# Float16 denominators with the queries split on GpSimd, and the output's sums of squares moved behind the split of qz

## Chip, cores and metric

One core of a Trainium2 chip. The metric is the device time of one execution in microseconds, lower is better; the kernel before takes 2459.85 us (median of three runs, 2457.72 to 2460.81). Engines are named as in the profile: PE is TensorE, PEld its weight load, DVE VectorE, ACT ScalarE, POOL GpSimd, SP the queue of SyncE.

## What is computed

x has 2 sequences of 4096 rows and 512 columns. First a linear attention with 16 heads of 32 columns, then a gated linear attention (GLA) with 8 heads of 64 and four sparse "experts"; both sit between layer norms and add to x.

```python
# first half, per head (d = e = 32, n = 4096)
q = relu(xn @ Wq.T); k = relu(xn @ Wk.T); v = xn @ Wv.T
ksum = k.sum(over n)
z = 1.0 / (einsum('bhd,bhdn->bhn', ksum, q) + eps)
context = einsum('bhdn,bhen->bhde', v, k)
out = einsum('bhde,bhen->bhdn', context, q) * z
x = x + layernorm(out @ Wproj.T + bproj)
# second half, per head, chunks of 64 rows: o = GLA(q1,k1,v,gk1) + sum over experts GLA(q2*e, k2*e, v, gk2*mask)
o = o * rsqrt(mean(o * o, axis=-1) + EPS) * norm_w
o = o * silu(g)
x = x + layernorm(o @ Wo)
```

The change touches the denominators ksum . q of the first half and the place of mean(o * o) in the second.

## The kernel before

A first stage (up to some 535 us) goes over 64 tiles of 128 rows in groups of four: layer norm, keys, queries and the moments that the context is made from. The queries, after their relu, are stored to q_cols in HBM as float32. Products of float32 accuracy with float16 operands are made by the helper `mm3` (L317 to L321): both operands are held as a high and a low float16 half, and three products (high-high, high-low, low-high) are added up in PSUM.

Between the stages VectorE makes `kden`: for each group of 128 columns the sums of the keys, spread over a block-diagonal 128x128 matrix in float32 (`key_totals`, `key_blocks`, L1463 to L1475). The weights of the mixing (`mix`) come from the context.

The second stage (from some 565 us to the end) goes over the 64 tiles again, in steps written out by hand for each engine (a `step` function per engine; loops of two steps). In step n, TensorE issues in this order: v of tile n, the sparse products of the GLA state for tile n-1 (`inter_sparse`, L494), the gates (L366), the dense ones and the intra-chunk products of n-1 (L503, L514), q1, k2, the output gate and k of n, then **the denominators of tile n+2** (`den`, L323 to L332), the output projection of tile n-2, the cumulated gates (L428, L429), q2, the half sums (L436, L438), **y of tile n+2** (`y_mm`, L334 and on; first instruction L336), the transposes of the gated q and k (L447), the state products (L466, L474), the routing and low-rank products of tile n+1 (a third use of `mm3`, 24 products of 128x128 by 128x128 for the low rank), and the scores of n (L457).

The way from the denominators to y, all of tile n+2 within step n: `den` on TensorE writes PSUM bank 0; ScalarE takes the logarithm and the exponential of it (`ahead_z`, L726 and L728); VectorE multiplies queries, key sums and that (`ahead_qz`, L1359) and splits the product into float16 halves (`ahead_qz_split`: L1181, L1183); `y_mm` reads those.

VectorE's order in a step: carries (L1220, L1229), router (L1264 and on), masks of the scores (L1200, L1208), masks of the cumulation, the low half of the low-rank values (L1255 to L1258), selection (L1239, L1242), join (L1247), log-sigmoids (L1298), maximum and difference for the softmax of k2 (L1319, L1325), `back_norm` (L1370: sums of the squares that ScalarE made at L816, per head, of tile n-1), the low half of the log-sigmoids (L1314), the output gate's log-sigmoid (L1304), the softmax's sum (L1329) and factor, the silu (L1310), qz and its split, the low half of xn (L1194), the gated q1, k1, q2 (L1341, L1342, L1348), the output row (L1376), the decay (L1353), and x1 of tile n+2 (L1190).

ScalarE in the same stretch: the output gate's logarithms (to L768), the exponential of k2 (L785), the sigmoid (L777, which waits for L1304), `ahead_z`, the four exponentials of the cumulated gates (to L795), `back_rms` (L820, which waits for L1370).

GpSimd in a step: the addition of the two score matrices (L1065), four masked copies of v (L1072), k2 times its factor (L1077), k2g (L1081, after ScalarE's L795), the state times the decay (L1088, L1089, after L1353), the output's norm and gate (L1096, L1100), the low half of the result (L1105). SyncE loads x and the queries of tile n+4 once x1 and qz of n+2 are done (buffers `xb`, `qb`, two each) and issues the transposing DMAs.

Of the kernel before, what the change touches and what calls it, by code (L numbers as in the profile page):

```python
# [4 lines left out]
BATCH, SEQ, C = 2, 4096, 512  # L5
# [41 lines left out]
def sandwich_kernel(nc, x_d, wqkv_d, wproj_d, bproj_d, wb_d, wl_d, ws_d, wo_d, nw_d, consts_d, out_d):  # L47
# [11 lines left out]
    with ExitStack() as ctx:  # L59
        def sb(name, *shape, dt=f32):  # L60
            return ctx.enter_context(nc.sbuf_tensor(name, [P, *shape], dt))
# [20 lines left out]
        mix = [sb("mix0", 2, KT, C, dt=f16), sb("mix1", 2, KT, C, dt=f16)]  # L82
        bias16 = sb("bias16", C, dt=f16)
        rk, ksum_q = sb("rk", BATCH, KT), sb("ksum_q", BATCH, KT)
        kden = sb("kden", BATCH, KT, P)


        region = sb("region", REGION)
# [100 lines left out]
        CREDITS = {  # L189
            "scalar": ["kh_ok", "q_read", "xh_ok",  # L190
                       "low1_ok", "labi_ok", "lexp_ok", "abs_ok", "ex_ok", "ln_ok", "sig_ok",
                       "v_ok", "ke_ok", "e1_ok", "e2_ok", "exs_ok", "q1T_ok", "k1T_ok", "q2T_ok", "k2T_ok",
                       "osq_ok", "z_ok", "ogh_ok", "xc_ok", "xnh_ok", "x1m_ok"],
            "vector": ["xn8_ok", "xf_ok", "kl_ok", "low_ok", "x1_ok", "xn_ok", "am1_ok", "am2_ok", "carry1_ok", "carry_ok", "ldiff_ok",
                       "same_ok", "osum_ok", "ls_ok", "lsl_ok", "sil_ok", "kd_ok", "k1g_ok", "q1g_ok", "q2g_ok",
# [10 lines left out]
        def cur(n):  # L206
            return n + 2
# [4 lines left out]
        def loads(n, p):  # L212
            return (n - p) * 8 + 16
# [97 lines left out]
        def _(pe):  # L311
# [9 lines left out]
                return mm(out, lhs(1), rhs(0), start=False, stop=stop)  # L321

            def den(n, p, b, at=0, back=True):  # L323
                pe.wait_ge(S(f"qb{p}_in"), loads(n, p))
                if at == 0:
                    pe.wait_ge(S("x1_ok"), prev(n))
                if back:
                    pe.wait_ge(S("sel_ok"), (n - 3) * 4 + 4)
                    pe.wait_ge(S("carry_ok"), n - 1)
                for g in range(KT):  # L330
                    last = mm(bank[at][:, g * P:(g + 1) * P], kden[:, b, g, :], qb[:, p, g, :], start=True, stop=True)  # L331
                last.then_inc(S("den_pe"), 1)  # L332

            def y_mm(n, b, at=0):  # L334
# [113 lines left out]
                    last.then_inc(S("tr_pe"), 1)  # L448

            def scores(n, path):  # L450
                kT, qT, where, k_ready, q_ready = ((k1T, q1T, (2, 5), "k1T_ok", "q1T_ok"), (k2T, q2T, (4, 6), "k2T_ok", "q2T_ok"))[path]
                pe.wait_ge(S(q_ready), cur(n))
                pe.wait_ge(S(k_ready), cur(n))
                for pr in range(PAIRS):
                    for odd in range(2):
                        h = slice(odd * D2, odd * D2 + D2)
                        last = mm(bank[where[odd]][:, pr * P:(pr + 1) * P], kT[h, pr, :], qT[h, pr, :], start=True, stop=True)  # L457
                last.then_inc(S("a_pe"), 1)
# [20 lines left out]

            def inter_sparse(n, front):  # L480
                pe.wait_ge(S("state_ok"), cur(n))
                pe.wait_ge(S("q2T_ok"), cur(n))
                pe.wait_ge(S("am1_ok"), cur(n))
                pe.wait_ge(S("carry_ok"), cur(n))
                if front:
                    pe.wait_ge(S("ldiff_ok"), cur(n + 1))
                for half in (1, 0):
                    if half == 0 and front:
                        pe.wait_ge(S("v_ok"), cur(n + 1))
                        pe.wait_ge(S("same_ok"), cur(n + 1))  # L490
                    for r in range(2):
                        for odd in range(2):
                            h = slice(odd * D2, odd * D2 + D2)
                            last = mm(psum[:, 2 * half + odd, r * 256:r * 256 + 256], q2T[h, 2 * half + r, :],  # L494
                                      statex[h, 2 * half + r, :], start=True, stop=True)
                last.then_inc(S("ix_pe"), 1)
# [121 lines left out]
                last.then_inc(S("ctx_pe"), 1)  # L618

            def mixing(b):  # L620
                pe.wait_ge(S("ctx_ok"), (6, 8)[b])
                pe.wait_ge(S("wproj_ok"), 1)
                if b == 0:
                    pe.wait_ge(S("moment_ok"), 2 * BATCH)
                else:
                    pe.wait_ge(S("mix_f_ok"), KT)
                for g in range(KT):
                    mm(bank[MIX_BANKS[b][g]], ctxT[b][:, g, :], wproj[:, g, :], start=True, stop=True).then_inc(S("mix_pe"), 1)
# [43 lines left out]
        def _(act):  # L672
# [14 lines left out]
                act.wait_ge(S(f"lnv{k}_ok"), n + 1)  # L687
                ac(rstd[:, k, :], lnv[:, k, :], ACT.Exp, scale=-0.5).then_inc(S(f"rstd{k}"), 1)

            def to_cols(n, dst, where, k, done):  # L690
                act.wait_ge(S("tr_pe"), n * 4 + 2 + k)
                ac(dst.rearrange("p a b -> p (a b)"), bank[where], ACT.Copy).then_inc(S(done), 1)  # L692

            def front_mean(n, p):
                act.wait_ge(S("xmean_ok"), n + 1)
# [107 lines left out]
            def front_transposed(n):  # L803
                act.wait_ge(S("inter_pe"), prev(n))
                act.wait_ge(S("a_pe"), n * 2 + 1)
                to_cols(n, q1T, 5, 0, "q1T_ok")
                to_cols(n, k1T, 2, 1, "k1T_ok")

            def front_transposed2(n):
                to_cols(n, q2T, 4, 2, "q2T_ok")  # L810
                to_cols(n, k2T, 6, 3, "k2T_ok")

            def back_square(n):
                act.wait_ge(S("osum_ok"), cur(n))
# [74 lines left out]
            def query(g, m):  # L889
                if m == 0:  # L890
                    act.wait_ge(S("q4_out"), g * (16 * GT) + 1)
                act.wait_ge(S("q_pe"), g * KT + m + 2)
                ac(q4[:, :, m, :], bank[3].rearrange("p (t c) -> p t c", t=GT), ACT.Relu,
                   scale=1.0 / W_SCALE).then_inc(S("q_read"), 1)

            def high(u, slot, moments_before=None):
                act.wait_ge(S("xf_ok"), cur(u))
# [28 lines left out]
                last.then_inc(S("moment_ok"), 1)  # L926

            def mixed(b):
                act.wait_ge(S("ctx_ok"), (6, 8)[b])
# [45 lines left out]
        def _(pool):  # L975
# [131 lines left out]
            def step(n, p, front=True, back=True):  # L1107
                if back:
                    back_am(n - 1)
                if front:  # L1110
                    front_vm(n, p)
                    front_k2(n)
                    front_state(n)
                if back:
                    back_gated(n - 1, 1 - p)
                    back_og_low(n - 1)
# [12 lines left out]
            for t in range(ALL):  # L1129
                add_keys(t, t // TILES)  # L1130
                if t in (3, 5):
                    load_weights((t - 3) // 2)
                if 8 <= t < 23:
                    late_piece(t - 8)
                if t == 23:
                    late_gates()
                    load_context_weights()
                if t in (27, 29):
                    centre_projection((t - 27) // 2)
            mix_late()  # L1140
            step(0, 0, back=False)
            with pool.Fori(1, ALL - 1, 2) as n:
                step(n, 1)
                step(n + 1, 0)
            step(ALL - 1, 1)
            step(ALL, 0, front=False)


        @block.vector
        def _(dve):  # L1150
# [227 lines left out]
            def step(n, p, b, front=True, back=True, tail=True, ahead=True, reset=False, late=True):  # L1378
# [20 lines left out]
                if front:  # L1399
                    front_logsig(n)  # L1400
                    front_kmax(n)
                    front_kdiff(n)
                if back:
                    back_norm(m)
                if front:
                    front_lslow(n)
                    front_out_logsig(n)
                    front_ksum(n)
                    front_kfac(n)
                    front_sil(n, p, tail)  # L1410
                if ahead:
                    ahead_qz(n + 2, p, b)
                    ahead_qz_split(n + 2)
                if late:
                    ahead_low(n + 1, mp)
                if front:
# [46 lines left out]
            def key_totals():  # L1463
                dve.wait_ge(S("ksum_pe"), BATCH)
                ve.tensor_scalar(flat(ksum_c[:, :, :]), bank[0][:, 0:BATCH * KT], 1.0 / W_SCALE, None, ALU.mult).then_inc(S("ctx_ok"), 1)
                dve.wait_ge(S("ctx_ok"), 1)
                key_blocks(0)
                ve.tensor_scalar(flat(ksum_q[:, :, :]), flat(ksum_c[:, :, :]), TINY, QZ_SCALE, ALU.max, ALU.mult).then_inc(S("ctx_ok"), 1)
                ve.tensor_scalar(flat(rk[:, :, :]), flat(ksum_c[:, :, :]), TINY, None, ALU.max).then_inc(S("ctx_ok"), 1)
                dve.wait_ge(S("ctx_ok"), 4)  # L1470
                ve.reciprocal(flat(rk[:, :, :]), flat(rk[:, :, :])).then_inc(S("ctx_ok"), 1)

            def key_blocks(b):
                ve.tensor_tensor(kden[:, b, :, :], blocks.unsqueeze(1).to_broadcast([P, KT, P]), wide(ksum_c[:, b, :], P),
                                 ALU.mult).then_inc(S("ctx_ok"), 1)  # L1475

            def context_blocks(b):
                dve.wait_ge(S("ctx_pe"), b + 1)
# [123 lines left out]
```

## Time and profile before

| what | value |
| --- | --- |
| three runs, median (lowest to highest) | 2459.85 us (2457.72 to 2460.81) |
| the profiled execution: its own time, its span | 2460.71 us, 2458.9 us |
| TensorE, matmul busy | 2400.0 us, 98% of the span |
| VectorE busy | 1805.9 us, 73% |
| ScalarE busy | 1580.2 us, 64% |
| GpSimd busy | 1136.8 us, 46% |
| granted TensorE clock, mean | 0.992 of full speed |

A line of code (L331) names a group of instructions. A matmul's busy time runs from its start to its modelled end, so that successive ones overlap; the distance of starts is what one costs in a row of its like. A float32 product appears as two records.

### The profile page before, as it was taken

What the parts mean: (1) busy time and instruction counts of PE and PEld (TensorE: products, weight loads), DVE (VectorE), ACT (ScalarE), POOL (GpSimd) and SP (SyncE); (2) the same over time, 40 slices, a digit from 0 to 9 for tenths busy, and PEclk for the clock granted to TensorE, in tenths of its full rate; (3) what the DMA queues carried; (4) which work ended last, traced back from release to release, by engine and by line L of the source; (5) the groups of instructions that cost most, each with busy time, mean ns of one, the idle gap of its engine ahead of it and who ended that gap; (6) DMA issues with size and microseconds to landing.
All of it is one profiled execution on the core that took longest, in us unless ns stands there. A gap on an engine that the chain in (4) does not pass through costs nothing.

```text
span 2458.9 us, 56923 instructions
## 1 busy us (share of the span) xinstructions
PE 2400.0 (98%) x20208; PEld 1433.9 (58%) x20208; DVE 1805.9 (73%) x3548; ACT 1580.2 (64%) x3473; POOL 1136.8 (46%) x929
## 2 busy tenths in 40 slices
PE   5999999998999999999999999999999999999997
PEld 2444444454666666666666666666666666666664
DVE  5444444426888888888888888888888888888885
ACT  3222323226777777777777777777777777777774
POOL 2587533313444444444444444444444444444444
PEclk9999999999999999999999999999999999999999
DMA  5634434311111111111111111111111111111111
GB/s 137 202 99 126 103 103 102 85 56 35 40 47 47 51 43 47 43 43 43 43 44 50 50 45 48 43 43 43 43 43 47 50 48 46 43 43 43 43 29 32
DMA packets 250704, 145.65 MB, mean 59 GB/s; under 512 B 208096, under 2 KB 208096, under 8 KB 250144
## 3 DMA queue, kind: packets, MB, share of 16 engines
q1 hardware_dynamic: 240048, 119.32, 19.6%
q10 hardware_dynamic: 9504, 17.31, 1.9%
q0 software_dynamic: 1104, 8.40, 0.9%
q8 instruction: 28, 0.46, 0.1%
q14 instruction: 20, 0.16, 0.0%
HBM read 61.09 MB, written 33.55 MB: 38 GB/s over the span
## 4 chain that ended last, share of the span: by engine, by line
PE 93%; POOL 3%; DVE 2%; ACT 1%; issue 1%; DMA 1%; POOLq 0%; SPq 0%; DVEq 0%; ACTq 0%
PE psum L319 17%; PE psum L320 16%; PE psum L321 16%; PE psum L592 6%; PE psum L457 5%; PE psum L494 5%; PE psum L447 4%; PE psum L474 4%; PE psum L503 3%; PE psum L514 2%; PE psum L331 2%; PE psum L368 2%; PE psum L367 2%; PE psum L466 2%; PE psum L366 1%; PE psum L429 1%
## 5 line engine op out<-in xcount | busy, mean ns | idle before, releaser
L319 PE MATMUL psum<-wb,region 128*128 128x512 f16 x768 | 293.0, 381 | 0.0
L320 PE MATMUL psum<-wb,region 128*128 128x512 f16 x768 | 291.6, 380 | 0.0
L321 PE MATMUL psum<-wb,region 128*128 128x512 f16 x768 | 291.6, 380 | 0.0
L1077 POOL TENSOR_TENSOR region<-region,kfac 128x512 f32<-128x512 f32 x64 | 66.7, 1042 | 482.9 <-DVE kfac L1335 482.9
L1060 POOL TENSOR_TENSOR region<-region 128x1024 f32<-128x1024 f32 x64 | 147.8, 2309 | 258.7 <-DVE region L1443 230.2
L1443 DVE SCALAR_TENSOR_TENSOR region<-psum,region 128x512 f16<-128x512 f32 x64 | 44.2, 691 | 222.4 <-ACT region L887 222.4
L1065 POOL TENSOR_TENSOR region<-region 128x1024 f32<-128x1024 f32 x64 | 150.5, 2352 | 93.2 <-DVE region L1208 93.2
L1072 POOL TENSOR_SCALAR region<-region,m 128x512 f32<-128x512 f32 x256 | 172.3, 692 | 26.5 <-DVE hm L1279 26.5
L592 PE MATMUL psum<-region 128*128 128x512 f16 x768 | 176.2, 379 | 2.1 <-DVE region L1443 2.1
L1081 POOL TENSOR_TENSOR region<-region 128x512 f32<-128x512 f32 x64 | 81.8, 1277 | 202.7 <-ACT region L795 202.7
L1242 DVE SCALAR_TENSOR_TENSOR region<-psum,m,region 128x512 f32<-128x512 f32 x192 | 144.1, 751 | 6.8
L781 ACT ACTIVATE region<-psum 128x512 f32<-128x512 f32 x64 | 38.2, 597 | 169.4 <-PE psum L321 169.4
L1439 DVE TENSOR_TENSOR region<-region 128x512 f16<-128x512 f32 x64 | 102.4, 1600 | 49.0 <-ACT region L900 49.0
L692 ACT ACTIVATE region<-psum 128x512 f32<-128x512 f32 x256 | 135.9, 582 | 0.0
L494 PE MATMUL psum<-region 64*128 64x256 f32 x1024 | 129.4, 393 | 2.7 <-DVE region L1200 2.7
L457 PE MATMUL psum<-region 64*128 64x128 f32 x2048 | 131.5, 278 | 0.0
L592 PEld LDWEIGHTS psum<-region 128*128 128x128 f16 x768 | 74.9, 98 | 93.5 <-DVE region L1443 3.6
L321 PEld LDWEIGHTS psum<-wb,region 128*128 128x128 f16 x768 | 75.3, 98 | 91.0 <-issue 0.6
L319 PEld LDWEIGHTS psum<-wb,region 128*128 128x128 f16 x768 | 75.0, 98 | 87.8 <-issue 0.6
L887 ACT ACTIVATE region<-psum 128x512 f16<-128x512 f32 x64 | 38.2, 597 | 136.2 <-PE psum L321 125.1
L447 PEld LDWEIGHTS psum<-cst,region 128*128 128x128 f32 x1024 | 115.9, 141 | 14.8 <-issue 2.5
L447 PE MATMUL psum<-cst,region 128*128 128x128 f32 x1024 | 123.0, 273 | 1.5 <-DVE region L1341 1.5
(236 smaller groups left out, 7208.3 us busy)
## 6 DMA issues: line engine op xcount, KB each, us to landing
region<-x_in SPq DMA_DIRECT2D x128, 256.0 KB, 2.6
q_cols<-region ACTq DMA_DIRECT2D x64, 256.0 KB, 2.5
region<-q_cols SPq DMA_DIRECT2D x64, 256.0 KB, 2.8
out_rows<-region SPq DMA_DIRECT2D x62, 256.0 KB, 2.0
region<-wb_in POOLq DMA_DIRECT2D x1, 3072.0 KB, 13.4
region<-wqkv_in SPq DMA_DIRECT2D x4, 512.0 KB, 6.9
region<-region SPq DMA_TRANSPOSE x128, 3.0
region<-ws_in POOLq DMA_DIRECT2D x1, 1280.0 KB, 7.6
```

What stands on the lines that cost most here:

```text
L319: mm(out, lhs(0), rhs(0), start=start, stop=False)
L320: mm(out, lhs(0), rhs(1), start=False, stop=False)
L321: return mm(out, lhs(1), rhs(0), start=False, stop=stop)
L447: last = nc.tensor.transpose(bank[where][:, g * P:(g + 1) * P], src[:, g * P:(g + 1) * P], ident)
L457: last = mm(bank[where[odd]][:, pr * P:(pr + 1) * P], kT[h, pr, :], qT[h, pr, :], start=True, stop=True)
L494: last = mm(psum[:, 2 * half + odd, r * 256:r * 256 + 256], q2T[h, 2 * half + r, :], statex[h, 2 * half + r, :], start=True, stop=True)
L592: last = mm(bank[4 + j], xn8[:, p * GT + t, x * C + j * P:x * C + (j + 1) * P], k16[:, y_, :], start=first and begins, stop=final and ends ...
L692: ac(dst.rearrange("p a b -> p (a b)"), bank[where], ACT.Copy).then_inc(S(done), 1)
L1060: nc.gpsimd.tensor_tensor(kacc[b], kacc[b], k16, ALU.add).then_inc(S("kacc_ok"), 1)
L1065: nc.gpsimd.tensor_tensor(am1[:, :, :, :], am1[:, :, :, :], am2[:, :, :, :], ALU.add).then_inc(S("am_ok"), 1)
L1072: last = nc.gpsimd.tensor_scalar(vm[:, e, :], v[:, p, :], m4[:, p, e:e + 1], 1.0, ALU.mult, ALU.mult)
L1242: ve.scalar_tensor_tensor(to, of[:, :, e, :], m4[:, p, e:e + 1], to, ALU.mult, ALU.add).then_inc(S("sel_ok"), 1)
```

## The change

The scale 1/64 is left off the relu of the queries, so that `q_cols` holds them 64 times as large, and the constants beside them are scaled to match. `kden` becomes two float16 matrices (high and low half of the key sums), made from `ks16` by VectorE. GpSimd splits each tile's queries into float16 halves `q16` with two instructions (`ahead_queries`), in step n for tile n+3, after k2g and before the state; the first three tiles are split before the first step. `den` uses `mm3` and waits for `q16_ok` in place of the load. On VectorE `back_norm` moves behind `ahead_qz_split`. The transposed copies of q and k on ScalarE signal once per path instead of once per copy, and TensorE waits once.

```diff
-        kden = sb("kden", BATCH, KT, P)
+        kden, ks16 = sb("kden", 2, BATCH, KT, P, dt=f16), sb("ks16", 2, BATCH * KT, dt=f16)
+        q16 = sb("q16", 2, 2, KT, P, dt=f16)
...
             def den(n, p, b, at=0, back=True):
-                pe.wait_ge(S(f"qb{p}_in"), loads(n, p))
+                pe.wait_ge(S("q16_ok"), n * 2 + 2)
...
                 for g in range(KT):
-                    last = mm(bank[at][:, g * P:(g + 1) * P], kden[:, b, g, :], qb[:, p, g, :], start=True, stop=True)
+                    last = mm3(bank[at][:, g * P:(g + 1) * P], lambda x: kden[:, x, b, g, :], lambda x: q16[:, p, x, g, :], True, True)
...
             def scores(n, path):
...
-                pe.wait_ge(S(q_ready), cur(n))
-                pe.wait_ge(S(k_ready), cur(n))
+                pe.wait_ge(S(ready), cur(n))
...
             def front_transposed(n):
...
-                to_cols(n, q1T, 5, 0, "q1T_ok")
-                to_cols(n, k1T, 2, 1, "k1T_ok")
+                to_cols(n, q1T, 5, 0)
+                to_cols(n, k1T, 2, 1).then_inc(S("path1_ok"), 1)
...
-                ac(q4[:, :, m, :], bank[3].rearrange("p (t c) -> p t c", t=GT), ACT.Relu,
-                   scale=1.0 / W_SCALE).then_inc(S("q_read"), 1)
+                ac(q4[:, :, m, :], bank[3].rearrange("p (t c) -> p t c", t=GT), ACT.Relu).then_inc(S("q_read"), 1)
...
+            def ahead_queries(n, p, again=True):
+                wait_alone(pool, S(f"qb{p}_in"), loads(n, p))
+                if again:
+                    wait_alone(pool, S("den_pe"), n)
+                nc.gpsimd.tensor_scalar(q16[:, p, 0], qb[:, p], 1.0, 1.0, ALU.mult, ALU.mult).then_inc(S("q16_ok"), 1)
+                pool.wait_ge(S("q16_ok"), n * 2 + 1)
+                nc.gpsimd.tensor_tensor(q16[:, p, 1], qb[:, p], q16[:, p, 0], ALU.subtract).then_inc(S("q16_ok"), 1)
+
...
                     front_k2(n)
+                if ahead:
+                    ahead_queries(n + 3, 1 - p)
+                if front:
                     front_state(n)
...
+            ahead_queries(0, 0, again=False)
+            ahead_queries(1, 1, again=False)
             mix_late()
+            ahead_queries(2, 0)
             step(0, 0, back=False)
...
                     front_kdiff(n)
-                if back:
-                    back_norm(m)
-                if front:
                     front_lslow(n)
...
                     ahead_qz_split(n + 2)
+                if back:
+                    back_norm(m)
...
                 dve.wait_ge(S("ctx_ok"), 1)
+                totals = flat(ksum_c[:, :, :])
+                ve.tensor_scalar(ks16[:, 0], totals, W_SCALE / SEQ, None, ALU.mult).then_inc(S("ctx_ok"), 1)
+                dve.wait_ge(S("ctx_ok"), 2)
+                ve.scalar_tensor_tensor(ks16[:, 1], totals, W_SCALE / SEQ, ks16[:, 0], ALU.mult, ALU.subtract).then_inc(S("ctx_ok"), 1)
...
             def key_blocks(b):
-                ve.tensor_tensor(kden[:, b, :, :], blocks.unsqueeze(1).to_broadcast([P, KT, P]), wide(ksum_c[:, b, :], P),
-                                 ALU.mult).then_inc(S("ctx_ok"), 1)
+                for x in range(2):
+                    last = ve.tensor_tensor(kden[:, x, b, :, :], blocks.unsqueeze(1).to_broadcast([P, KT, P]),
+                                            wide(ks16[:, x, b * KT:(b + 1) * KT], P), ALU.mult)
+                last.then_inc(S("ctx_ok"), 1)
```

## Rows read from the trace of the kernel before

**Rows 1.** The page, part 1: busy us, share of the span, instructions.
```profile
PE 2400.0 (98%) x20208; PEld 1433.9 (58%) x20208; DVE 1805.9 (73%) x3548; ACT 1580.2 (64%) x3473; POOL 1136.8 (46%) x929
```

**Rows 2.** Stretch: length; busy us of PE, PEld, DVE, ACT, POOL; PEclk, DMA share, GB/s.
```profile
1200.00:1800.00 600.00, 600.00 (x5741) 382.30 (x5738) 499.16 (x1028) 456.58 (x1015) 284.20 (x247) 1.00 0.18 46
```

**Rows 3.** TensorE's waits, whole span: total us, times, longest us.
```profile
PE psum L336 <- DVE region L1183: 5.3, 3, 1.9
```

**Rows 4.** Timeline of TensorE, step at 1225: start us, us, engine, line.
```profile
1225.07 1.05 PE L331 MATMUL psum<-region,kden 128*128 128x128 f32 x8
1225.96 0.38 PE L319 MATMUL psum<-wo,ogT 128*128 128x512 f16 x1
...
1229.85 0.19 PE L436 MATMUL psum<-halves,region 128*128 128x2 f16 x2
...
1230.32 0.39 PE L336 MATMUL psum<-bias,ones 128*128 128x512 f16 x1
```

**Rows 5.** Timeline of VectorE, the same step.
```profile
1223.59 0.67 DVE L1370 TENSOR_REDUCE oms<-region 128x8 f32<-128x512 f32 x1
...
1225.31 0.68 DVE L1304 SCALAR_TENSOR_TENSOR region<-psum,region 128x512 f32<-128x512 f32 x1
...
1229.57 0.69 DVE L1183 TENSOR_TENSOR region<-region 128x512 f16<-128x512 f32 x1
1230.18 0.75 DVE L1194 SCALAR_TENSOR_TENSOR region<-region,rstd 128x512 f16<-128x512 f32 x1
```

**Rows 6.** The chain that ended last, in order of time: scores of successive steps.
```profile
1209.93 1.99 PE psum L457 x32
...
1239.14 1.99 PE psum L457 x32
...
1268.26 1.99 PE psum L457 x32
```

**Rows 7.** Timeline of TensorE: first and last of a tile's 24 low-rank products.
```profile
1208.43 0.22 PE L319 MATMUL psum<-region,wl 128*128 128x128 f16 x1
...
1209.71 0.22 PE L321 MATMUL psum<-region,wl 128*128 128x128 f16 x1
```

**Rows 8.** Timeline of ScalarE, step at 1225.
```profile
1224.21 0.63 ACT L768 ACTIVATE region<-region 128x512 f32<-128x512 f32 x1
...
1226.03 0.63 ACT L777 ACTIVATE region<-region 128x512 f32<-128x512 f32 x1 [0.67 <-DVE region L1304]
1226.56 0.64 ACT L726 ACTIVATE psum<-psum,eps_z 128x512 f32<-128x512 f32 x1
```

**Rows 9.** Groups of instructions of GpSimd: busy us, mean ns, idle before.
```profile
L1105 POOL TENSOR_TENSOR og<-og 128x512 f16<-128x512 f32 x64 | 74.1, 1157 | 102.2 <-ACT og L828 102.2
...
L1010 POOL TENSOR_SCALAR region<-region,wsum 128x512 f32<-128x512 f32 x4 | 8.8, 2210 | 0.3
...
L1015 POOL TENSOR_SCALAR bias<-bproj 128x512 f16<-128x512 f32 x1 | 0.6, 617 | 0.1
```

**Rows 10.** Timeline of GpSimd, between k2g and the state.
```profile
1202.34 1.27 POOL L1081 TENSOR_TENSOR region<-region 128x512 f32<-128x512 f32 x1 [3.25 <-ACT region L795]
1204.84 1.05 POOL L1088 TENSOR_TENSOR region<-region,decay 128x512 f32<-128x512 f32 x1 [1.23 <-DVE decay L1353]
```

**Rows 11.** Timelines of VectorE and TensorE: carries, router, low rank, gates.
```profile
1208.23 0.86 DVE L1220 TENSOR_TENSOR region<-psum,region 64x256 f32<-64x256 f32 x2 [1.45 <-PE psum L474]
...
1210.98 0.16 DVE L1264 TENSOR_REDUCE lmax<-psum 128x1 f32<-128x4 f32 x1 [0.57 <-ACT region L737]
...
1215.73 0.29 DVE L1258 SCALAR_TENSOR_TENSOR region<-psum,region 64x128 f16<-64x128 f32 x1
...
1216.53 0.60 PE L366 MATMUL psum<-ws,region 128*128 128x512 f16 x2
```

**Rows 12.** Timelines of VectorE and GpSimd in the second step.
```profile
615.94 1.75 DVE L1194 SCALAR_TENSOR_TENSOR region<-region,rstd 128x512 f16<-128x512 f32 x1
...
615.74 1.41 POOL L1081 TENSOR_TENSOR region<-region 128x512 f32<-128x512 f32 x1 [1.66 <-ACT region L795]
```

More of the change, by code:

```diff
@@ L191, in sandwich_kernel @@
                        "low1_ok", "labi_ok", "lexp_ok", "abs_ok", "ex_ok", "ln_ok", "sig_ok",
-                       "v_ok", "ke_ok", "e1_ok", "e2_ok", "exs_ok", "q1T_ok", "k1T_ok", "q2T_ok", "k2T_ok",
+                       "v_ok", "ke_ok", "e1_ok", "e2_ok", "exs_ok", "path1_ok", "path2_ok",
                        "osq_ok", "z_ok", "ogh_ok", "xc_ok", "xnh_ok", "x1m_ok"],
@@ L450, in scores @@
             def scores(n, path):
-                kT, qT, where, k_ready, q_ready = ((k1T, q1T, (2, 5), "k1T_ok", "q1T_ok"), (k2T, q2T, (4, 6), "k2T_ok", "q2T_ok"))[path]
-                pe.wait_ge(S(q_ready), cur(n))
-                pe.wait_ge(S(k_ready), cur(n))
+                kT, qT, where, ready = ((k1T, q1T, (2, 5), "path1_ok"), (k2T, q2T, (4, 6), "path2_ok"))[path]
+                pe.wait_ge(S(ready), cur(n))
                 for pr in range(PAIRS):
@@ L481, in inter_sparse @@
                 pe.wait_ge(S("state_ok"), cur(n))
-                pe.wait_ge(S("q2T_ok"), cur(n))
+                pe.wait_ge(S("path2_ok"), cur(n))
                 pe.wait_ge(S("am1_ok"), cur(n))
@@ L620, in mixing @@
             def mixing(b):
-                pe.wait_ge(S("ctx_ok"), (6, 8)[b])
+                pe.wait_ge(S("ctx_ok"), (8, 10)[b])
                 pe.wait_ge(S("wproj_ok"), 1)
@@ L688, in rstd_of, with to_cols @@
                 ac(rstd[:, k, :], lnv[:, k, :], ACT.Exp, scale=-0.5).then_inc(S(f"rstd{k}"), 1)
-            def to_cols(n, dst, where, k, done):
+            def to_cols(n, dst, where, k):
                 act.wait_ge(S("tr_pe"), n * 4 + 2 + k)
-                ac(dst.rearrange("p a b -> p (a b)"), bank[where], ACT.Copy).then_inc(S(done), 1)
+                return ac(dst.rearrange("p a b -> p (a b)"), bank[where], ACT.Copy)
             def front_mean(n, p):
@@ L805, in front_transposed @@
                 act.wait_ge(S("a_pe"), n * 2 + 1)
-                to_cols(n, q1T, 5, 0, "q1T_ok")
-                to_cols(n, k1T, 2, 1, "k1T_ok")
+                to_cols(n, q1T, 5, 0)
+                to_cols(n, k1T, 2, 1).then_inc(S("path1_ok"), 1)
             def front_transposed2(n):
-                to_cols(n, q2T, 4, 2, "q2T_ok")
-                to_cols(n, k2T, 6, 3, "k2T_ok")
+                to_cols(n, q2T, 4, 2)
+                to_cols(n, k2T, 6, 3).then_inc(S("path2_ok"), 1)
             def back_square(n):
@@ L928, in mixed @@
             def mixed(b):
-                act.wait_ge(S("ctx_ok"), (6, 8)[b])
+                act.wait_ge(S("ctx_ok"), (8, 10)[b])
                 for g in range(KT):
@@ L1105, in back_og_low, with step @@
                 nc.gpsimd.tensor_tensor(og16[:, 1, :], og[:, :], og16[:, 0, :], ALU.subtract).then_inc(S("og_ok"), 1)
-            def step(n, p, front=True, back=True):
+            def ahead_queries(n, p, again=True):
[5 more added lines that the diff above has]
+                nc.gpsimd.tensor_tensor(q16[:, p, 1], qb[:, p], q16[:, p, 0], ALU.subtract).then_inc(S("q16_ok"), 1)
+            def step(n, p, front=True, back=True, ahead=True):
                 if back:
@@ L1139, in _ @@
                     centre_projection((t - 27) // 2)
+            ahead_queries(0, 0, again=False)
+            ahead_queries(1, 1, again=False)
             mix_late()
+            ahead_queries(2, 0)
             step(0, 0, back=False)
-            with pool.Fori(1, ALL - 1, 2) as n:
+            with pool.Fori(1, ALL - 3, 2) as n:
                 step(n, 1)
                 step(n + 1, 0)
-            step(ALL - 1, 1)
-            step(ALL, 0, front=False)
+            step(ALL - 3, 1, ahead=False)
+            step(ALL - 2, 0, ahead=False)
+            step(ALL - 1, 1, ahead=False)
+            step(ALL, 0, front=False, ahead=False)
         @block.vector
@@ L1466, in key_totals @@
                 dve.wait_ge(S("ctx_ok"), 1)
+                totals = flat(ksum_c[:, :, :])
+                ve.tensor_scalar(ks16[:, 0], totals, W_SCALE / SEQ, None, ALU.mult).then_inc(S("ctx_ok"), 1)
+                dve.wait_ge(S("ctx_ok"), 2)
+                ve.scalar_tensor_tensor(ks16[:, 1], totals, W_SCALE / SEQ, ks16[:, 0], ALU.mult, ALU.subtract).then_inc(S("ctx_ok"), 1)
+                dve.wait_ge(S("ctx_ok"), 3)
                 key_blocks(0)
-                ve.tensor_scalar(flat(ksum_q[:, :, :]), flat(ksum_c[:, :, :]), TINY, QZ_SCALE, ALU.max, ALU.mult).then_inc(S("ctx_ok"), 1)
+                ve.tensor_scalar(flat(ksum_q[:, :, :]), flat(ksum_c[:, :, :]), TINY, QZ_SCALE / W_SCALE, ALU.max, ALU.mult).then_inc(S("ctx_ok"), 1)
                 ve.tensor_scalar(flat(rk[:, :, :]), flat(ksum_c[:, :, :]), TINY, None, ALU.max).then_inc(S("ctx_ok"), 1)
-                dve.wait_ge(S("ctx_ok"), 4)
+                dve.wait_ge(S("ctx_ok"), 6)
                 ve.reciprocal(flat(rk[:, :, :]), flat(rk[:, :, :])).then_inc(S("ctx_ok"), 1)
             def key_blocks(b):
-                ve.tensor_tensor(kden[:, b, :, :], blocks.unsqueeze(1).to_broadcast([P, KT, P]), wide(ksum_c[:, b, :], P),
-                                 ALU.mult).then_inc(S("ctx_ok"), 1)
+                for x in range(2):
+                    last = ve.tensor_tensor(kden[:, x, b, :, :], blocks.unsqueeze(1).to_broadcast([P, KT, P]),
+                                            wide(ks16[:, x, b * KT:(b + 1) * KT], P), ALU.mult)
+                last.then_inc(S("ctx_ok"), 1)
             def context_blocks(b):
```

## The prediction

> **What bounds the kernel now.** I read the page first: TensorE is busy for 2400.0 us, 98% of the span [rows 1]. A matmul's busy time overlaps the next one's here, so I read the second half by stretches: from 1200 to 1800 us TensorE is busy for 600.00 of 600 us at a granted clock of 1.00, the upper of its two levels (2.4 GHz), while VectorE has 499 us, ScalarE 457 and GpSimd 284 [rows 2]. Then the waits: those of TensorE that bear on this change are three for L1183, the split of qz, 5.3 us together, all before 620 us [rows 3]. So in the 62 steps that look two tiles ahead, TensorE's own instruction stream sets the period, and what it issues less is gained, as long as no other engine becomes late.
>
> One wait is too short for that view. In the step at 1225 us the half sums begin at 1229.85 and need eight pairs, the last of which should let y start at about 1230.25; y (L336) starts at 1230.32, just after VectorE's L1183 ends at 1229.57 + 0.69 = 1230.26 [rows 4, 5]. The scores of three successive steps start at 1209.93, 1239.14 and 1268.26 [rows 6]: 29.21 us, then 29.12. So every second step already loses some 0.07 us to qz. The reader should see two things: TensorE is the bound, and qz stands right behind it.
>
> **The change, part by part.**
>
> Denominators. Removed are eight records of L331 per tile (four products, each as two float32 passes): from 1225.07 to the next product at 1225.96, 0.89 us or 111 ns apiece [rows 4]. Added are 12 products with float16 operands of the same 128x128 by 128x128 shape. The low-rank products are that shape and in the same helper: the 24 of one tile start between 1208.43 and 1209.71, 23 intervals, 55.7 ns each [rows 7]. Twelve make 0.67 us, so a step saves 0.22 us. Bounds: 111 ns apiece, were the type to save nothing, would make 1.33 us, 0.44 us a step lost; 55.7 ns is the other end. I take 55.7, since shape, type, operand sources and pattern match.
>
> y earlier. The saving is worth something only if qz is earlier too: in the new order of time TensorE wants qz at 1230.03 in this step. Today's chain [rows 5, 8]: VectorE's sum of squares L1370 (1223.59, the next instruction 0.59 later), L1314 (1.2 us), L1304 at 1225.31, ScalarE's L777 waiting for it until 1226.03, L726 at 1226.56, L728, VectorE's L1359 at 1227.95, the split until 1230.26. With L1370 out of the way, L1314 starts at 1223.59 and L1304 would be free at 1224.7; it then waits for ScalarE's L768, 1224.21 + 0.63 = 1224.84, and starts at 1224.9, 0.41 earlier. L777 moves to 1225.6 (the exponential before it ends at 1225.35), L726 to 1226.15 (the denominators end by then: 1225.74 plus the 0.2 us that a result takes to come out), qz is ready at 1229.85. That is 0.18 us before TensorE wants it. Margin: thin, but positive. The 0.07 us of every second step is won back as well.
>
> The moved sum. L1370 (0.67 us) now stands between the split and L1194, so what follows on VectorE starts at 1230.4 instead of 1230.18 and, against a TensorE that is 0.22 us ahead, 0.4 us later. Behind it are queued L1194 (the low half of xn: its transpose has 6 us until the next step's routing), the gated q and k, and the output. Who waits for its result: ScalarE's back_rms, at 1231.27 today and 1231.05 then; the sum ends at 1230.45, 0.6 us ahead. Nothing. The gated queries end at 1231.7; the transposes stand behind y's 13 wide products and want them 2.8 us after 1230.03. Nothing. TensorE waits for one semaphore instead of two in two places and ScalarE signals less: nothing, the ScalarE copies themselves stay.
>
> The split of the queries on GpSimd, between k2g and the state. A conversion and a subtraction of 128x512 per tile. Nearest rows: L1015, a multiply with float16 output, 617 ns; L1105, a subtraction with float16 output, 1157 ns [rows 9]. With two hand-overs that is 1.9 us. The upper bound for the first is L1010, a tensor-scalar of the same size at 2210 ns [rows 9]; I take L1015, because operation, types and operands without a vector are its own, and L1010 subtracts a column. Cover: GpSimd idles 1.23 us there, from the end of k2g at 1203.61 until the state L1088 at 1204.84 [rows 10]. So the state moves from 1204.84 to 1205.55, 0.7 us later, ending at about 1208.5 instead of 1207.8. The carries on VectorE (L1220, today held to 1208.23 by TensorE) start 0.3 us late; they have 0.57 us of idle before L1264 [rows 11], which waits for ScalarE. Covered, and behind it the gates on TensorE (L366, 1216.53) have another 0.51 us over L1258, which ends at 1216.02 [rows 11]. The loads it waits for are issued a step and more earlier, and its result is used a step later. GpSimd's output chain behind the state ends 0.7 us later, before a transpose with 13 us to spare.
>
> A rule to weigh. In the second step VectorE's L1194, which reads two tensors of SBUF, took 1.75 us, begun at 615.94 while GpSimd's L1081 ran from 615.74 to 617.15; in the step at 1225 us, with GpSimd idle beside it, it takes 0.75 [rows 5, 12]. So two such instructions hold each other up. The Trainium skill, "SBUF — State Buffer", § Who interferes with whom, calls it an exclusive lock: a VectorE instruction with two SBUF inputs blocks fully while a GpSimd instruction that reads SBUF runs. By that rule, with which this row agrees, the small product L1353 (decay) would stand still behind the new subtraction.
>
> In rows: L1353 is due at 1204.5 and would end near 1205.7 instead of 1204.76; the state then starts at 1205.8, 0.96 us later than today, and the carries 0.55 us late, just within the 0.57. So with or without this the sum is the same; the spare beneath it is not.
>
> Edges. Before the first step, the denominators of tiles 0 and 1 save 0.22 us each, but TensorE then waits 5.3 us in three places for L1183 [rows 3], which hangs on the mixing weights: nothing. VectorE's two small products and the doubled key blocks (four times 0.69 instead of twice) lie in waits of some 5 us on TensorE's context products. On GpSimd the queries of tiles 0 and 1 are split beneath those products; tile 2 comes after the mixing weights and delays the first masked values by about 0.1 us, which nobody waits for. Step 0: saving swallowed by its wait for qz. Step 1, of that kind too, gets the 0.5 us by which qz comes earlier. The tail has no queries: nothing.
>
> **Sum.** 60 steps of 0.22 are 13.2; 30 of 0.07 are 2.1; step 1 gives 0.5; edges 0.1 lost: 15.7 us. Against the profiled execution's own time, 2460.7 us, that is 2445.0; it lies 0.9 us above the median of the three runs, 2459.85, so I state 2444.1.
>
> **Rivals.**
>
> (a) y waits on. If the chain to qz moves by less than the 0.22 us, say because L726 or L768 is later than I have it, what is gained is what qz gains: half of 0.41 us leaves 0.2 us a step, and 0.1 us leaves 6 us in all, 2453. For it: a margin of 0.18 us and a chain over three engines. Against it: each link was read off a row.
>
> (b) Nothing gained. The 0.22 us turns into a wait, at qz (if ScalarE's order kept it where it is) or by a float16 product that costs more behind a wide one than in a row of its like. Time 2457 to 2462. The low-rank rows speak against the second part.
>
> (c) Slower, on the state. The mechanism is GpSimd's pair standing before the state. Price: with 2.21 + 1.16 + 0.1 = 3.5 us the state comes 2.3 us late, the carries 1.9, L1264 1.3 and the gates 0.8 us after TensorE wants them: 62 x 0.8 = 50 less 15.7, so 34 us slower, 2494. It decides from a pair of 2.7 us (1.9 + 0.27 left before L1264 + 0.51 before the gates). For it: L1010, a tensor-scalar of this size [rows 9]. Against: the two rows that share operation and types.
>
> (d) The lock at L1194. If L1194 were to start after GpSimd's k2g (as it did in step 1) it would end 1.3 us late each step and hold the gated queries; TensorE would lose about that, 62 x 1.3 = 81, less 15.7: 2525. L1194 starts at 1230.4, k2g at 1231.25: 0.85 us of spare, so this is unlikely.
>
> **Chances.** Forecast 0.66; (a) 0.13; (b) 0.09; (c) 0.08; (d) 0.04. About 0.2%, 5 us, is what a measurement of this kernel can tell from no change. Faster by more than that: forecast and (a), 0.79; within: 0.09; slower: 0.12. The range takes the forecast, 2 us to either side for the spread of runs, and (a) up to 2454: 2442 to 2454.
>
> **What would show it.** L331 is gone; in its place stand 12 float16 products of some 220 ns in 0.67 us. Scores start every 28.90 us in both kinds of step. y starts with no gap behind the half sums, and L1359 about 0.4 us earlier against the start of the denominators. GpSimd's new pair takes 1.8 to 1.9 us, and the state starts 0.7 to 1.0 us later against k2g. VectorE's idle time before the router's maximum shrinks from 0.57 us to almost none. Wrong would be: TensorE waiting at y for L1183's successor (a), at the gates or at the sparse products for VectorE (c), at the transposes (d), or denominators over 0.8 us (b).

## The result and the profile after

The changed kernel takes 2441.73 us (median of four runs, 2440.76 to 2443.98) against 2460.22 of the kernel before, measured beside it; the ratio is 0.993, with an interval of 0.9919 to 0.9942. In the later comparisons, with 21 and 15 more runs, the kernel before had medians of 2458.7 and 2458.8 us. So the change is worth 17 to 18.5 us. The profiled execution took 2440.76 us.

The page, part 1, of the changed kernel (the answer to [rows 1]), and the stretch from 1200 to 1800 us, columns as in [rows 2]:

```profile
PE 2381.8 (98%) x20464; PEld 1410.8 (58%) x20464; DVE 1853.0 (76%) x3552; ACT 1580.8 (65%) x3473; POOL 1249.4 (51%) x1057
```
```profile
1200.00:1800.00 600.00, 600.00 (x5837) 377.18 (x5834) 522.19 (x1042) 459.33 (x1012) 318.01 (x289) 1.00 0.17 44
```

TensorE is still busy for the whole of that stretch. VectorE has 23 us more in it, though the change adds no instruction to its steps; the experiments come back to that. The chain that ended last shows the scores of three successive steps, as [rows 6] did:

```profile
1171.27 1.99 PE psum L457 x32
1200.17 1.99 PE psum L457 x32
1229.08 1.99 PE psum L457 x32
```

They are 28.90 and 28.91 us apart: the step is 0.26 us shorter on average, and the difference between the two kinds of step (29.21 and 29.12 before) is gone. TensorE's timeline in the step at 1215 us, beside [rows 4]:

```profile
1215.32 0.22 PE L320 MATMUL psum<-q,kden 128*128 128x128 f16 x1
...
1215.93 0.22 PE L322 MATMUL psum<-q,kden 128*128 128x128 f16 x1
1215.99 0.38 PE L320 MATMUL psum<-wo,ogT 128*128 128x512 f16 x1
...
1219.88 0.19 PE L437 MATMUL psum<-halves,region 128*128 128x2 f16 x2
...
1220.28 0.38 PE L337 MATMUL psum<-bias,ones 128*128 128x512 f16 x1
```

The first product of the output projection follows the first float16 product of the denominators by 0.67 us, where it was 0.89. Half sums begin at 1219.88 and y at 1220.28, 0.40 us later; before, it was 1229.85 to 1230.32, 0.47. So 0.40 us is what eight pairs take when nothing holds up y. VectorE and ScalarE in that step, beside [rows 5, 8]:

```profile
1215.12 0.69 DVE L1319 SCALAR_TENSOR_TENSOR region<-psum,region 128x512 f32<-128x512 f32 x1
...
1217.78 1.12 DVE L1374 SCALAR_TENSOR_TENSOR region<-region,ksum_q,psum 128x128 f32<-128x128 f32 x4 [0.27 <-ACT psum L728]
...
1219.39 0.69 DVE L1198 TENSOR_TENSOR region<-region 128x512 f16<-128x512 f32 x1
1220.00 0.68 DVE L1385 TENSOR_REDUCE oms<-region 128x8 f32<-128x512 f32 x1
...
1223.77 0.86 DVE L1368 TENSOR_TENSOR decay<-exs 128x20 f32<-128x20 f32 x1
```
```profile
1214.46 0.63 ACT L768 ACTIVATE region<-region 128x512 f32<-128x512 f32 x1
...
1215.85 0.63 ACT L777 ACTIVATE region<-region 128x512 f32<-128x512 f32 x1 [0.24 <-DVE region L1319]
1216.39 0.64 ACT L726 ACTIVATE psum<-psum,eps_z 128x512 f32<-128x512 f32 x1
...
1221.27 0.32 ACT L820 ACTIVATE oln<-oms,zero_eps 128x8 f32<-128x8 f32 x1
```

The split of qz ends at 1220.08, 4.76 us after the denominators began; before it was 1230.26 less 1225.07, 5.19. Between the split's end and y there are now 0.20 us in this kind of step, and 0.31 us in the one that follows it. The sum of squares now follows it (L1385), and the last VectorE row is the decay product, 0.86 us for 20 elements per partition. GpSimd, beside [rows 10], then the carries and the router beside [rows 11]:

```profile
1221.49 1.27 POOL L1080 TENSOR_TENSOR region<-region 128x512 f32<-128x512 f32 x1 [3.45 <-ACT region L795]
1222.74 0.61 POOL L1110 TENSOR_SCALAR q<-region 128x512 f16<-128x512 f32 x1
1223.43 1.16 POOL L1112 TENSOR_TENSOR q<-region,q 128x512 f16<-128x512 f32 x1
1224.71 1.05 POOL L1087 TENSOR_TENSOR region<-region,decay 128x512 f32<-128x512 f32 x1
```
```profile
1198.82 0.86 DVE L1235 TENSOR_TENSOR region<-psum,region 64x256 f32<-64x256 f32 x2 [1.80 <-POOL region L1088]
...
1201.23 0.16 DVE L1279 TENSOR_REDUCE lmax<-psum 128x1 f32<-128x4 f32 x1 [0.23 <-ACT region L737]
...
1205.97 0.29 DVE L1273 SCALAR_TENSOR_TENSOR region<-psum,region 64x128 f16<-64x128 f32 x1
```
```profile
1206.77 0.60 PE L367 MATMUL psum<-ws,region 128*128 128x512 f16 x2
```

The state starts 1.95 us after the end of k2g (1222.76) instead of 1.23; the carries now wait for it (1.80 us, released by GpSimd's L1088); the router's idle time is down from 0.57 to 0.23 us; the gates keep their 0.51 us over L1273 (which ends at 1206.26).

### The profile page after: what moved, and what is told of

The parts are those of the page before. It is cut to its first block, busy times and chain, and to the rows that moved or that the text cites. A ratio compares the mean times of both kernels' runs of the same rounds, so it can differ in the third digit from the quotient of the medians.

```text
span 2438.9 us, 57678 instructions
## 1 busy us (share of the span) xinstructions
PE 2381.8 (98%) x20464; PEld 1410.8 (58%) x20464; DVE 1853.0 (76%) x3552; ACT 1580.8 (65%) x3473; POOL 1249.4 (51%) x1057
## 4 chain that ended last, share of the span: by engine, by line
PE 92%; POOL 3%; DVE 2%; issue 1%; ACT 1%; DMA 1%; POOLq 0%; SPq 0%; DVEq 0%; ACTq 0%
PE psum L320 18%; PE psum L321 17%; PE psum L322 17%; PE psum L592 6%; PE psum L457 5%; PE psum L494 5%; PE psum L448 4%; PE psum L474 4%; PE psum L503 3%; PE psum L514 2%; PE psum L369 2%; PE psum L368 2%; PE psum L466 2%; PE psum L367 1%; PE psum L429 1%
## 5 line engine op out<-in xcount | busy, mean ns | idle before, releaser
L1235 DVE TENSOR_TENSOR region<-psum,region 64x256 f32<-64x256 f32 x126 | 53.2, 422 | 115.6 <-POOL region L1088 110.4
```

## Experiments

**The denominators alone.** The sum of squares goes back to its old place.

```diff
                     front_kdiff(n)
+                if back:
+                    back_norm(m)
+                if front:
                     front_lslow(n)
...
                     ahead_qz_split(n + 2)
-                if back:
-                    back_norm(m)
```

> The whole change, but VectorE's sum of squares stays at its old place ahead of the low half of the log-sigmoids. Theory (qz stands right behind TensorE): in the kernel before, y starts 0.02 to 0.10 us after the split of qz ends, and that chain hangs on VectorE and ScalarE, not on the denominators. So the 0.22 us saved per step turns into a wait or a gap ahead of y, and only the 0.0 to 0.1 us of today's slack is gained: period 29.10 us or so against 28.91 in the changed kernel, time 2455 to 2459 us. Rival (TensorE alone is the bound): the 13 us of the denominators come in full, period 28.95, time 2446 to 2449 us.

Measured: 2458.77 us (11 runs), ratio to the kernel before 1.000, 0.9991 to 1.0009. Its steps, TensorE at y, and VectorE's way there:

```profile
1179.07 1.99 PE psum L457 x32
1208.17 1.99 PE psum L457 x32
1237.38 1.99 PE psum L457 x32
```
```profile
1227.87 0.19 PE L437 MATMUL psum<-halves,region 128*128 128x2 f16 x2
...
1228.56 0.39 PE L337 MATMUL psum<-bias,ones 128*128 128x512 f16 x1
```
```profile
1223.56 0.68 DVE L1319 SCALAR_TENSOR_TENSOR region<-psum,region 128x512 f32<-128x512 f32 x1
...
1227.81 0.69 DVE L1198 TENSOR_TENSOR region<-region 128x512 f16<-128x512 f32 x1
```

The period is 29.10 and 29.21 us, as if nothing had been changed, with 0.22 us less work in it. Half sums to y is 0.69 us where 0.40 are needed: y is 0.29 us late, 0.06 us behind the split, which ends at 1228.50. In the other kind of step it is 0.19 us late. The view of waits shows no row for this at all between 640 and 2330 us, because the records of the half sums run on (0.19 us each) over most of the gap. The distance of starts shows it. The theory holds, at the end of its range where nothing is gained.

**The moved sum alone.** The kernel before, with `back_norm` behind `ahead_qz_split`, as in the change.

> The kernel before, with nothing changed but the place of the sum of squares (behind the split of qz). Theory: TensorE's stream is untouched; only the 0.07 us that every second step loses at y comes back, some 2 us, and a little in the second step: period 29.12 us in all steps, time 2456 to 2459 us, L1359 about 0.4 us earlier against the start of the denominators. Rival (the move is the larger part of the gain): time under 2450 us.

Measured: 2455.52 us (11 runs), ratio 0.9984, 0.9975 to 0.9993, half a microsecond better than expected. Its steps:

```profile
1178.17 1.99 PE psum L457 x32
1207.30 1.99 PE psum L457 x32
1236.42 1.99 PE psum L457 x32
```

29.13 and 29.12 us: the 0.08 us that nearly every other step lost is back, 2.2 us over the 59 steps from the third on. In the two profiled executions another 1.9 us lies before the third step; the section on the prediction comes back to that. So one part alone gives 0, the other 3.2, and both together 17: the two are not a sum. The move makes the room in which the denominators' saving can be had. From this kernel to the change the step falls by 0.22 us (29.13 to 28.91), which is just what the denominators give (0.89 to 0.67); that leaves nothing for the joined signals of the transposed copies, which no run here tries alone.

**One more conversion on GpSimd**, ahead of the pair.

```diff
+        spare = sb("spare", 1, KT, P, dt=f16)
...
+                nc.gpsimd.tensor_scalar(spare[:, 0], qb[:, p], 1.0, 1.0, ALU.mult, ALU.mult)
                 nc.gpsimd.tensor_scalar(q16[:, p, 0], qb[:, p], 1.0, 1.0, ALU.mult, ALU.mult).then_inc(S("q16_ok"), 1)
```

> The changed kernel, with one more conversion of the queries (0.62 us, into a spare tile) ahead of GpSimd's pair. Theory A (my rival c: what decides are the gates): the state and the carries come 0.6 us later, 0.22 us of it is idle time before the router's maximum, 0.4 of the 0.51 us ahead of the gates is used, TensorE waits nowhere: 2441 to 2443 us. Theory B (the delay travels on along VectorE: the log-sigmoids L1313, on which ScalarE's copies and logarithms hang, come 0.4 us later, and with them qz, which has 0.2 us of slack): TensorE loses about 0.18 us at y in each of 60 steps, 11 us, time 2450 to 2455 us. Theory C (GpSimd has room everywhere): 2441 to 2443, with the gates' slack unchanged.

Measured: 2442.87 us (5 runs), ratio 0.9931, 0.9918 to 0.9945, against the change's 0.993. VectorE and then TensorE (lines are one or two further down here: L1281 is the router's maximum, L1275 the last low half, L368 the gates):

```profile
1205.53 0.15 DVE L1281 TENSOR_REDUCE lmax<-psum 128x1 f32<-128x4 f32 x1
...
1210.22 0.29 DVE L1275 SCALAR_TENSOR_TENSOR region<-psum,region 64x128 f16<-64x128 f32 x1
```
```profile
1210.96 0.60 PE L368 MATMUL psum<-ws,region 128*128 128x512 f16 x2
```

The time is that of theories A and C, and the steps are 28.91 us apart as in the change. The path is that of none of them in full. The state comes 0.43 us later against k2g than in the change (median 2.38 us after it, for 1.95), not 0.6. The router has no idle time left, as A has it, but the gates keep 0.45 us of their 0.51, where A left them 0.11. And the delay does travel on towards y, as B has it: it takes 0.1 us a step off VectorE's wait for the product of k2 (18.8 us in the changed kernel between 640 and 2330 us, 12.8 here), and the split of qz ends 0.10 us nearer to y (0.10 and 0.20 us before it in the two kinds of step, for 0.20 and 0.31). At this size that is still covered, so B's loss of 0.18 us a step does not come.

**Two more conversions.** As before, with `spare` of two tiles and both written.

> The changed kernel with two more conversions of the queries (1.24 us, into spare tiles) ahead of GpSimd's pair. With one more, the router's maximum had no idle time left, the gates 0.45 us of slack and y 0.10 us. So another 0.65 us of delay has to show. Theory A (the gates alone decide): TensorE loses 0.2 us a step, 12 us, 2453 to 2457 us. Theory B (the delay travels on over the log-sigmoids to qz and decides at y): 0.65 less the 0.10 of y and at most 0.21 idle time before the softmax's maximum, 0.35 to 0.55 us a step, 21 to 33 us, 2463 to 2475 us. Theory C (room everywhere): 2442 us.

Measured: 2460.41 us (11 runs), ratio 1.0007, 0.9998 to 1.0016: 18.7 us more than the changed kernel. TensorE's waits between 640 and 2330 us, its timeline, and VectorE's (L1276 last low half, L1322 the output gate's log-sigmoid, L1201 the split of qz):

```profile
PE psum L338 <- DVE region L1201: 5.3, 26, 0.2
```
```profile
1213.38 0.61 PE L368 MATMUL psum<-ws,region 128*128 128x512 f16 x2
...
1226.48 0.19 PE L438 MATMUL psum<-halves,region 128*128 128x2 f16 x2
...
1227.23 0.39 PE L338 MATMUL psum<-bias,ones 128*128 128x512 f16 x1 [0.20 <-DVE region L1201]
```
```profile
1213.03 0.29 DVE L1276 SCALAR_TENSOR_TENSOR region<-psum,region 64x128 f16<-64x128 f32 x1
...
1222.22 0.69 DVE L1322 SCALAR_TENSOR_TENSOR region<-psum,region 128x512 f32<-128x512 f32 x1 [0.48 <-ACT region L769]
...
1226.48 0.69 DVE L1201 TENSOR_TENSOR region<-region 128x512 f16<-128x512 f32 x1
```

The gates start 0.06 us after the low half ends at 1213.32. They are just held up, as y is at that distance from its split; but the product before them stands only 0.01 to 0.03 us further ahead of them than in the change, so hardly anything is paid there. Half sums to y is 0.75 us, 0.35 too many, and 0.65 in the other kind of step. VectorE's log-sigmoids are late, ScalarE's logarithms with them, and L1322 waits 0.48 us for those. The steps are 0.32 us longer than the change's on average (29.23 for 28.91). This is theory B's path, at a price below its range (0.35 to 0.55 us a step, 2463 to 2475 us): a late state is paid at y, one engine further than my rival (c) had it. The view of waits lists only 26 steps, though the distances show y held up in nearly all.

**The pair in GpSimd's gap.**

```diff
                     front_vm(n, p)
-                    front_k2(n)
                 if ahead:
                     ahead_queries(n + 3, 1 - p)
                 if front:
+                    front_k2(n)
                     front_state(n)
```

> The changed kernel, with GpSimd's pair moved into its idle time of 7 us between the masked values and k2's factor. Theory: the state starts right after the decay again, 0.6 to 0.7 us earlier against k2g; the decay product L1353 (L1368 in the changed kernel) takes 0.17 us instead of 0.88, since no GpSimd instruction that reads SBUF runs beside it; VectorE's idle time before the router's maximum is back at about 0.5 us; all of it was covered, so the time stays: 2440 to 2443 us. Rival (the lock and the late state cost something already): 2 to 5 us faster, 2437 to 2439 us.

Measured: 2441.07 us (5 runs), ratio 0.9926, 0.9912 to 0.9939: the same as the change within the spread. The decay product in the changed kernel and in this one (count, then ns: minimum, median, maximum):

```profile
L1368 DVE TENSOR_TENSOR decay<-exs x64: 163/883/908, 584.7 to 2405.9; 128x20 f32<-128x20 f32 x64
```
```profile
L1368 DVE TENSOR_TENSOR decay<-exs x64: 164/171/172, 585.5 to 2406.7; 128x20 f32<-128x20 f32 x64
```

From 883 to 171 ns. What it took in the changed kernel was a stall: it began at 1223.77 and ended at 1224.63, where GpSimd's subtraction had run from 1223.43 to 1224.59. Over the whole execution this one line grew from 10.8 to 52.9 us busy, which is 42 of the 47 us by which VectorE's busy time rose (1805.9 to 1853.0). None of it reached TensorE: the steps are 28.91 us apart in both kernels. I take this placement as the better one all the same: it leaves the router 0.57 us of idle time instead of 0.23. It has brought no time in any run here.

**Fewer products for the denominators.** First without the key sums' low half (8 products), then with the two high halves alone (4 products). These leave out the corrections named, and so part of the accuracy of z.

```diff
-                    last = mm3(bank[at][:, g * P:(g + 1) * P], lambda x: kden[:, x, b, g, :], lambda x: q16[:, p, x, g, :], True, True)
+                    out = bank[at][:, g * P:(g + 1) * P]
+                    mm(out, kden[:, 0, b, g, :], q16[:, p, 0, g, :], start=True, stop=False)
+                    last = mm(out, kden[:, 0, b, g, :], q16[:, p, 1, g, :], start=False, stop=True)
```

> The changed kernel without the product of the key sums' low half (8 products instead of 12 for the denominators; that correction is left out). TensorE issues another 0.22 us less per step, while qz stays where it is, since ScalarE's logarithm follows its sigmoid and not the denominators. Theory (the next bound is qz, with 0.20 to 0.32 us of slack by the steps looked at): 0.20 to 0.22 us a step, 12 to 13 us, 2428 to 2430 us, y right behind the split of qz. Rival (the slack has gone to measurement or the chain moves with the denominators' length): nothing or the same 13 us with the slack unchanged.

> As before, with only the product of the two high halves (4 products; both corrections are left out). TensorE issues 0.45 us less per step than in the changed kernel. Theory (qz bounds): only the slack of 0.20 to 0.32 us is gained, 12 to 19 us in all, 2423 to 2430 us, and y waits 0.15 to 0.25 us a step. Rival (TensorE's stream alone): 27 us, 2414 to 2416 us.

Measured: 2432.05 us (4 runs; ratio 0.989, 0.9874 to 0.9905) and 2431.76 us (4 runs; 0.9887, 0.9872 to 0.9902), each some 2 us above the range expected. The first 0.22 us of TensorE's work is worth 9.7 us, the second nothing. With two products per group the scores are 28.78 and 28.69 us apart:

```profile
1171.05 1.99 PE psum L459 x32
1199.74 1.99 PE psum L459 x32
1228.52 1.99 PE psum L459 x32
```

28.69 is 28.91 less the 0.22; in every second step qz is in the way again. With one product per group the steps are 28.78 and 28.67 us, and TensorE at y, and ScalarE:

```profile
1215.41 0.39 PE L332 MATMUL psum<-q,kden 128*128 128x128 f16 x4
...
1220.22 0.39 PE L337 MATMUL psum<-bias,ones 128*128 128x512 f16 x1 [0.16 <-DVE region L1198]
```
```profile
1215.93 0.63 ACT L777 ACTIVATE region<-region 128x512 f32<-128x512 f32 x1 [0.24 <-DVE region L1319]
1216.47 0.64 ACT L726 ACTIVATE psum<-psum,eps_z 128x512 f32<-128x512 f32 x1
```

Four products begin at 1215.41, and their records end at 1215.80. ScalarE's logarithm starts 0.67 us after that, at 1216.47, the moment its sigmoid L777 lets go of the engine (successive instructions start 0.54 us apart there). So the chain to qz hangs on ScalarE's queue and VectorE, not on the denominators, and the slack at qz is all that the change left.

That slack is smaller than I had counted, which is why both times lie above their ranges. I took 0.20 to 0.32 us, from the end of the split to y. But wherever y is held up it starts 0.06 us after the split (1228.50 to 1228.56 above, 1227.17 to 1227.23), so only 0.14 and 0.25 us can be had in the two kinds of step, 0.20 on average. The steps got shorter by 0.18 us on average with eight products (0.22 us in the kind with 0.25 to give, 0.13 in the other) and by 0.19 with four.

**Eight products and the pair in the gap**, the two edits above together.

> Eight products for the denominators (the key sums' low half is left out) and GpSimd's pair in its idle gap before k2's factor. Theory: as with the pair before the state, 2427 to 2430 us, since neither the decay product's stall nor the later state is on the way to qz. Rival (the freed time on VectorE reaches qz too): under 2426 us.

Measured: 2431.7 us (4 runs), ratio 0.9888, 0.9873 to 0.9903, some 2 us above the range expected, as the two before. Some 10 us faster than the change, by leaving out the product with the key sums' low half; the placement adds nothing to it.

## Why the prediction was right

Forecast 2444.1 us in a range of 2442.0 to 2454.0; the measured median, 2441.73, is 2.4 us better and 0.3 us below the range's lower end. (Taken as the ratio, 0.993 of the 2459.85 us that the forecast started from, it is 2442.6.) The gain is 18.5 us by the medians side by side, and 17.0 or 17.1 against the larger sets of runs of the kernel before; forecast 15.7. Faster was given 0.79. The mechanism is shown by the experiments; what the sum lacks is 1 to 3 us at the edges, and it is these that took the time just past the range's end. Part of them comes and goes between profiled executions, so how near the number came is in part luck.

- Denominators: 0.67 us forecast from the low-rank rows, 0.67 measured.
- y and qz: that qz stands right behind TensorE, and that the saving is worth something only if qz is earlier too, is what the first experiment shows. L1304 (now L1319) starts earlier, and L777 and L726 with it: the split ends 4.76 us after the denominators begin, forecast 4.78. The spare before y, 0.20 us in this step, was forecast as 0.18; by the 0.06 us above, 0.14 of it could be used.
- The steps: 28.90 forecast, 28.91 measured. Over the 59 steps from the third on that is 15.2 us, where the sum had 15.3: 13.0 of it from the denominators and 2.2 from the lost 0.08 us.
- The moved sum: nothing, and that holds; ScalarE's L820 starts at 1221.27, after the sum's end at 1220.68.
- GpSimd's pair: 1.9 us forecast, L1110 0.61 and L1112 1.16 with a hand-over, state after 1.95. The decay's stall came as forecast, ending at 1224.63 with the subtraction.
- Router: "almost none" was forecast under the lock, 0.23 us is left. The state is 0.72 us later against k2g, not 0.96: L1368 ends 0.04 us after the subtraction, where I had nearly its whole 0.17 us follow it, and the pair took 1.83 us instead of 1.9.
- Edges: this is the term that was mis-sized. I had 0.5 us for the second step and nothing before it. The two profiled executions differ by 20 us, more than the medians, and in them the third step's scores start 4.9 us earlier in the changed kernel: 2.4 us lie before the first step's scores, 2.2 in the second step (30.8 us before, 28.6 after), 0.3 in the step between.
- The part before the first step. The rows show a granted clock of 0.83 on average between 530 and 570 us before, 0.91 after. But the kernels with one more conversion and with the pair in the gap have 0.84 and 0.83 there with the change in place. So this part comes and goes, and the forecast had no reason to hold it.
- The second step. y waits 1.9 to 2.0 us for qz in all kernels, and then some run it partly at the clock's lower level (1.2 GHz: wide products 0.43 us apart), some wholly at the upper (2.4 GHz: 0.22). Granted on average between 600 and 625 us: 0.93 in the kernel before, the denominators alone, and eight and four products (the step is 30.3 to 30.8 us there); 1.00 in the change, the moved sum alone, the three with other work on GpSimd, and eight products with the pair in the gap (28.6 to 28.7 us). It is worth some 2 us, once. Each is one profiled execution, and what tips it stays open.

Rival (a), y waiting on, did not occur at 12 products but sets in at once behind them. Rival (c) has its mechanism right and its place wrong: the pair could take 0.6 us more free of charge and costs 19 us at 1.24 more, and y is where nearly all of it is paid, not the gates.

## What to carry to other kernels

Where one engine is busy without a gap, look for the operand that arrives just in time behind it: work taken off the engine is worth only the slack of that operand, and a reordering elsewhere that frees a few tenths of a microsecond can be worth nothing alone and everything together. Read such slack from the distance of starts, since a view of waits built on records that overlap can show nothing of it (0.2 to 0.3 us in every step here). Count it down to the shortest distance at which the reader was ever seen to start behind the operand (0.06 us here), not down to zero. And where there is a choice, put an instruction that reads SBUF on GpSimd where GpSimd is idle for long, rather than ahead of something that others wait for; here it saved idle time on another engine and no time.

## What the runs showed that I had not expected

- Gaps of 0.2 to 0.3 us ahead of y in every step (the denominators alone), with no row in the waits.
- 0.62 us more on GpSimd ahead of the state moved the state by 0.43. The decay product, which stalled beside the subtraction in the changed kernel, got through before it here. GpSimd and VectorE of that kernel:

```profile
1227.50 0.62 POOL L1112 TENSOR_SCALAR q<-region 128x512 f16<-128x512 f32 x1
1228.21 1.17 POOL L1114 TENSOR_TENSOR q<-region,q 128x512 f16<-128x512 f32 x1
```
```profile
1228.05 0.17 DVE L1370 TENSOR_TENSOR decay<-exs 128x20 f32<-128x20 f32 x1
```

The decay starts at 1228.05 and is through in 0.17 us, as the subtraction begins at 1228.21. So the same two instructions cost 0.7 us of VectorE or nothing, by which of them starts first. The Trainium skill, "SBUF — State Buffer", § Who interferes with whom, states that the order of issue, not the kind of instruction, decides who is held up. The two traces agree with it: 0.86 us where GpSimd's subtraction started first, 0.17 where the decay did. With two more conversions the decay fell behind a conversion instead, begun 0.15 us before it, and took 0.49 us (median), to that conversion's end.
- The clock's level in the second step: behind the same wait of 1.9 us, some profiled executions lose 2 us and others nothing.
